# Attention and a routed expert layer in one program: the Router's chain in pieces between heads, halving on GpSimd, fewer row sends in the drain

## The reference, cut to what matters

```python
x = layernorm(x + attention(x))          # 16 heads, softmax(q k^T / sqrt(8)) v, then Wo, bo
# expert layer on N = 4096 tokens
shared = gelu(xf @ Wfc_s + bfc_s) @ Wproj_s + bproj_s
probs = softmax(xf @ Wr)                 # 8 experts
topk_p, topk_i = top_k(probs, 2); topk_p /= sum(topk_p)
routed = sum over the 2 chosen e: topk_p * (gelu(xf @ Wfc[e] + bfc[e]) @ Wproj[e] + bproj[e])
x = layernorm(x + shared + routed)
```

## Time and profile before

| | us |
|---|---|
| median of 3 runs | 584.2 |
| lowest and highest | 571.56, 597.54 |
| profiled execution, its own time | 578.29 |
| its span, first to last instruction | 576.5 |
| mean granted TensorE clock in it | 0.845 of full speed |

### The profile page before, as it was taken

How to read it: one execution, slowest core, us unless ns; L and a number is a source line. 1 busy time by engine, 2 the same in 40 slices (tenths; PEclk the granted TensorE clock), 3 DMA queues, 4 the chain that set the end, 5 groups by cost and what they waited for, 6 DMA issues and landing times. The chain is left out here.

```text
span 576.5 us, 14294 instructions
## 1 busy us (share of the span) xinstructions
PE 454.4 (79%) x5135; PEld 305.8 (53%) x5135; DVE 387.3 (67%) x873; ACT 306.9 (53%) x546; POOL 310.1 (54%) x417
## 2 busy tenths in 40 slices
PE   5998899989989887899992469991899999996000
PEld 2444454444545443344551358980699999995000
DVE  3658766696888787877721186550598999985095
ACT  1158755786888773545760366770444554452035
POOL 5322764466666631434678407881066666667185
PEclk9999956797999895656997589995899999999555
DMA  3234414453554431222121101114911111110263
GB/s 91 67 101 141 138 57 127 125 158 109 159 149 115 122 103 43 70 62 71 56 73 42 42 1 52 46 44 115 261 43 44 48 43 40 37 34 23 95 233 109
DMA packets 63127, 50.29 MB, mean 87 GB/s; under 512 B 7354, under 2 KB 54596, under 8 KB 63060
## 3 DMA queue, kind: packets, MB, share of 16 engines
q1 hardware_dynamic: 58516, 40.91, 25.4%
q0 software_dynamic: 4544, 8.47, 4.6%
HBM read 24.96 MB, written 22.95 MB: 83 GB/s over the span
## 5 line engine op out<-in xcount | busy, mean ns | idle before, releaser
L540 DVE TENSOR_REDUCE row_max<-s_ps 128x2 f32<-128x512 f32 x256 | 165.2, 684 | 57.4 <-PE s_ps L677 55.2
L400 ACT ACTIVATE probs<-ring_ps 128x1024 f32<-128x1024 f32 x128 | 130.9, 1023 | 76.5 <-PE ring_ps L695 76.2
L1573 POOL DMA_INDIRECT results<-gated,dest x78 | 78.8, 1010 | 63.3 <-DVE gated L1674 50.2
L677 PE MATMUL s_ps<-qk_stack 24*128 24x256 f16 x512 | 96.1, 302 | 18.7 <-DVE row_max L540 12.2
L1645 ACT ACTIVATE hid_r<-h_ps_r,bias 128x256 f32<-128x256 f32 x156 | 61.1, 474 | 74.5 <-PE h_ps_r L1309 74.5
L695 PE MATMUL ring_ps<-qk_stack 26*128 26x256 f16 x512 | 95.7, 303 | 0.0
L1276 POOL DMA_INDIRECT slots<-rows,slot_at x64 | 70.5, 1101 | 38.3 <-issue 17.5
L713 PE MATMUL av_ps<-probs,v_aug 128*32 128x256 f32 x1024 | 84.5, 457 | 0.0
L677 PEld LDWEIGHTS s_ps<-qk_stack 24*128 24x128 f16 x512 | 37.9, 99 | 79.0 <-issue 37.0
L310 POOL TENSOR_SCALAR max_scaled<-row_max 128x16 f32<-128x16 f32 x32 | 6.6, 205 | 104.2 <-DVE row_max L540 103.9
L1321 PE MATMUL y_ps_r<-w,hid_r 128*128 x312 | 58.1, 220 | 0.0
(11 more groups left out here) (208 smaller groups left out, 1060.3 us busy)
## 6 DMA issues: line engine op xcount, KB each, us to landing
qk_stack<-qk_rows SPq DMA_DIRECT2D x64, 96.0 KB
slots<-empty_row SPq DMA_DIRECT2D x13, 390.0 KB, 5.2
qk_rows<-qk_parts SPq DMA_DIRECT2D x16, 256.0 KB, 2.6
experts<-results SPq DMA_DIRECT2D x8, 512.0 KB, 6.9
rows_in<-slots SPq DMA_DIRECT2D x3, 1040.0 KB, 11.2
w_stage<-in_w_fc SPq DMA_DIRECT2D x9, 256.0 KB, 3.1
w_stage<-in_w_proj SPq DMA_DIRECT2D x9, 256.0 KB, 3.7
x_t<-in_x_t SPq DMA_DIRECT2D x16, 128.0 KB, 2.3
```

Source lines behind the costliest of these rows:

```text
L400: nc.scalar.activation(probs[:, n % PROBS], ring(key), ACT.Exp, scale=SCORE_SCALE).then_inc(ring_emptied, 1)
L540: nc.vector.tensor_reduce(row_max[:, h], s1_ps[:, h % 2], AX_X, ALU.max, negate=True).then_inc(max_done, 1)
L677: mm = nc.tensor.matmul(s1_ps[:, h % 2, t], band_of(q_stack, b, h, TERM_ROWS)[:, t * P:(t + 1) * P], band_of(k_stack, b, h, TERM_ROWS), st ...
L1573: nc.gpsimd.indirect_dma_start(out=a["results"][:, :], out_offset=bass.IndirectOffsetOnAxis(ap=dest[:, t.buf, half:half + 1], axis=0), in_ ...
```

## The change

1. The chain for share 0 is cut into pieces of one to four instructions and put between pairs of heads: `find`, `mark`, `settle` (together the old `pick`) for both choices in step 13; `tally`, `claim`, `offset` (the old `reserve`), `order`, `jump` (the old `rank`) and `gate` in step 14; `place(0, 0)`, `place(0, 1)`, `shift_on` and `end_on` (the old `move_on`) in step 15. `gap` is now made after `chosen`. PE's count moves from p = 6 of step 13 to p = 1 of step 14, ACT's `take_counts` and `share_gap` to step 14.
2. `make_x1` multiplies by 64: the variance with its eps is scaled by 1/4096 before the power of -1/2. So `x1_all` holds 64 x1. `cut_rows` needs no factor and moves to POOL, at the end of odd steps 5 to 19, all eight groups. The shared sum divides by `W_UNIT`, as do the gates, and the last layer norm's eps is multiplied by 4096.
3. Loads, casts and splits of the nine experts' weights are at listed steps, the shared expert's first: casts in 3, 4, 5, 7, 9, 11, 12, 13, 15, splits one later for each.
4. 17 instead of 30 sends stand in the attention block (3 in step 15, 5 in 16, 5 in 17, 4 in 18, none in 19), 47 instead of 34 in `share_and_place`.
5. In steps 13 to 16, PE runs `keep_clock(2)` after `project_v` (p = 2) and at p = 6.

```diff
-COUNT_STEPS = {13: 0}
+PICK_STEP, COUNT_STEP, PLACE_STEP = 13, 14, 15
-PLACED = {14: (0, 2), 15: (2, 2), 16: (2, 2), 17: (2, 4), 18: (4, 4), 19: (4, 2)}
+PLACED = {15: (0, 3), 16: (2, 3), 17: (2, 3), 18: (2, 2)}
+WEIGHT_ORDER = (8, 0, 1, 2, 3, 4, 5, 6, 7)
+CAST_AT = (3, 4, 5, 7, 9, 11, 12, 13, 15)
+SPLIT_AT = (4, 5, 6, 8, 10, 12, 13, 14, 16)
+LOAD_AT = (2, 3, 4, 6, 8, 10, 11, 12, 14)
+KEPT = range(13, 17)
...
 def halved_in(t):
-    return turned_in(t + 1)
+    g = (t - 5) // 2
+    return g if t % 2 == 1 and 0 <= g < GROUPS else None
...
             def make_x1(b):
-                nc.gpsimd.tensor_scalar(var_eps[:], mean_var[:, :, 1], EPS, None, ALU.add).then_inc(scale_done, 1)
+                nc.gpsimd.tensor_scalar(var_eps[:], mean_var[:, :, 1], EPS, X_UNIT ** -2, ALU.add, ALU.mult).then_inc(scale_done, 1)
...
             (POOL's step)
                 if last.exists():
                     add_bias(last)
+                if halved_in(t) is not None:
+                    halve(halved_in(t))
                 placer.send(PLACED.get(t, (0, 0))[1])
...
             (DVE's step, after heads 0 to 3 and take_mean)
-                if t in COUNT_STEPS:
-                    logits_taken(COUNT_STEPS[t])
-                    router.pick(COUNT_STEPS[t], 0)
-                if t == 14:
+                if now.exists():
+                    largest(now, 4)
+                    largest(now, 5)
+                if t == PICK_STEP:
+                    logits_taken(0)
+                    router.find(0, 0)
+                if t == COUNT_STEP:
                     counts_taken(0)
-                    router.reserve(0)
+                    router.tally(0)
+                if t == PLACE_STEP:
+                    router.place(0, 0)
                 if now.exists():
-                    for h in range(4, 8):
-                        largest(now, h)
...
+                    largest(now, 6)
+                    largest(now, 7)
+                if t == PICK_STEP:
+                    router.mark(0)
+                if t == COUNT_STEP:
+                    router.claim(0)
+                if t == PLACE_STEP:
+                    router.place(0, 1)
                 if last.exists():
                     invert_sums(last)
                     normalise(last)
...  (then, after heads 9, 11, 13 and 15:
      step 13: settle(0, 0); find(0, 1); mark(0); settle(0, 1)
      step 14: offset(0); order(0); jump(0); gate(0)
      step 15: shift_on(0); end_on(0))
...
             (PE's step)
+                    if p == COUNT_AT and t == COUNT_STEP:
+                        count(0)
...
                         project_v(now)
-                        if not last.exists():
+                        if not last.exists() or t in KEPT:
                             keep_clock(2)
...
                             turn_heads(last)
-                        elif now.exists():
+                        if now.exists() and (t in KEPT or not last.exists()):
                             keep_clock(2)
...
-def cut_rows(nc, dve, a, g):
+def cut_rows(nc, pool, a, g):
     tiles = slice(g * GROUP, (g + 1) * GROUP)
     parts = a["rows1"][:].bitcast(F16)
-    nc.vector.tensor_scalar(parts[:, tiles, 0:D], a["x1_all"][:, tiles], X_UNIT, 1.0, ALU.mult, ALU.mult)\
-      .then_inc(a["x_high"], 1)
-    dve.wait_ge(a["x_high"], g + 1)
-    nc.vector.scalar_tensor_tensor(out=parts[:, tiles, D:2 * D], in0=a["x1_all"][:, tiles], scalar=X_UNIT,
-                                   in1=parts[:, tiles, 0:D], op0=ALU.mult, op1=ALU.subtract).then_inc(a["x_low"], 1)
+    nc.gpsimd.tensor_scalar(parts[:, tiles, 0:D], a["x1_all"][:, tiles], 1.0, 1.0, ALU.mult, ALU.mult).then_inc(a["x_high"], 1)
+    pool.wait_ge(a["x_high"], g + 1)
+    nc.gpsimd.tensor_tensor(parts[:, tiles, D:2 * D], a["x1_all"][:, tiles], parts[:, tiles, 0:D], ALU.subtract)\
+      .then_inc(a["x_low"], 1)
...
             (share_and_place, DVE)
-            cut_rows(nc, dve, a, LAST_GROUP)
             low(0)
```

More of the change, by code:

```diff
@@ L365, in split_biases, with halve @@
                 pool.wait_ge(a["weights_low"], 2)
+            def halve(g):
+                pool.wait_ge(x1_made, 4 * g + 4)
+                cut_rows(nc, pool, a, g)
             placer = Placer(nc, pool, a)
@@ L473, in step @@
                     exp_pair(late, 1)
+                if t == COUNT_STEP:
+                    take_counts(0)
+                if late.exists():
                     evacuate_max(late, 1)
@@ L621, in step @@
                 if now.exists():
[L622 to L628, removed]
-                if halved_in(t) is not None:
-                    halve(halved_in(t))
-                if now.exists():
-                    for h in range(12, HEADS):
-                        largest(now, h)
+                    largest(now, 8)
+                    largest(now, 9)
+                if t == PICK_STEP:
+                    router.settle(0, 0)
+                if t == COUNT_STEP:
+                    router.offset(0)
+                if t == PLACE_STEP:
+                    router.shift_on(0)
+                if now.exists():
+                    largest(now, 10)
+                    largest(now, 11)
+                if t == PICK_STEP:
+                    router.find(0, 1)
+                if t == COUNT_STEP:
+                    router.order(0)
+                if t == PLACE_STEP:
+                    router.end_on(0)
+                if now.exists():
+                    largest(now, 12)
+                    largest(now, 13)
+                if t == PICK_STEP:
+                    router.mark(0)
+                if t == COUNT_STEP:
+                    router.jump(0)
+                if now.exists():
+                    largest(now, 14)
+                    largest(now, 15)
+                if t == PICK_STEP:
+                    router.settle(0, 1)
+                if t == COUNT_STEP:
+                    router.gate(0)
             run_steps(step)
@@ L1168, in pick, with mark, settle @@
         TE = [P, n, EXPERTS]
[L1169 removed]
+        best, score = a["best"][:, :, 0:n], a["score"][:, 0:n]
         of = a["logits"][:, tiles] if k == 0 else a["rest"][:, 0:n]
         if k == 1:
[L1172 removed]
+            then(nc.vector.scalar_tensor_tensor(out=of, in0=a["hot"][:, 0, tiles], scalar=FAR_BELOW, in1=a["logits"][:, tiles],
                                                 op0=ALU.mult, op1=ALU.add))
         then(nc.vector.tensor_reduce(best[:, k], of, AX_X, ALU.max))
[L1175 to L1176 removed]
         then(nc.vector.tensor_tensor(score, of, best[:, k].unsqueeze(2).to_broadcast(TE), ALU.is_equal))
[L1178 to L1180 removed]
+    def mark(self, c):
+        nc, a, then = self.nc, self.a, self.then
+        n = SHARES[c][1] - SHARES[c][0]
+        score, first = a["score"][:, 0:n], a["first"][:, 0:n]
+        then(nc.vector.tensor_tensor(score, score, a["from_end"][:].unsqueeze(1).to_broadcast([P, n, EXPERTS]), ALU.mult))
+        then(nc.vector.tensor_reduce(first, score, AX_X, ALU.max))
+    def settle(self, c, k):
+        nc, a, then = self.nc, self.a, self.then
+        tiles, n = slice(*SHARES[c]), SHARES[c][1] - SHARES[c][0]
+        hot, best, score, first = a["hot"], a["best"][:, :, 0:n], a["score"][:, 0:n], a["first"][:, 0:n]
+        then(nc.vector.tensor_tensor(hot[:, k, tiles], score, first.unsqueeze(2).to_broadcast([P, n, EXPERTS]), ALU.is_equal))
         if k == 1:
             then(nc.vector.tensor_tensor(a["chosen"][:, tiles], hot[:, 0, tiles], hot[:, 1, tiles], ALU.add), a["chosen_made"])
+            then(nc.vector.tensor_tensor(a["gap"][:, tiles], best[:, 1], best[:, 0], ALU.subtract), a["gap_made"])
+    def pick(self, c, k):
+        self.find(c, k)
+        self.mark(c)
+        self.settle(c, k)
     def gate(self, c):
@@ L1189, in gate @@
         dve.wait_ge(a["gap_exp"], c + 1)
-        then(nc.vector.tensor_scalar(gate1, exp_gap, UNIT, UNIT, ALU.mult, ALU.add))
+        then(nc.vector.tensor_scalar(gate1, exp_gap, W_UNIT, W_UNIT, ALU.mult, ALU.add))
         then(nc.vector.reciprocal(gate1, gate1))
@@ L1231, in rank @@
         then(nc.vector.tensor_tensor(rank, rank, over, ALU.add))
+    def rank(self, c):
+        self.order(c)
+        self.jump(c)
     def place(self, c, k):
@@ L1248, in move_on, with end_on @@
         then(nc.vector.tensor_tensor(a["shift"][:, c + 1], a["shift"][:, c], more[:], ALU.add))
+    def end_on(self, c):
+        nc, a, then = self.nc, self.a, self.then
+        some, more = a["some"], a["more"]
         then(nc.vector.scalar_tensor_tensor(out=more[:], in0=a["passing"][:, c], scalar=float(BLOCK), in1=some[:], op0=ALU.mult,
```

121 lines of the change are left out of this document (59 added, 62 removed).

## The result

| | us |
|---|---|
| median before, 4 runs | 581.03 (571.56 to 597.54) |
| median after, 4 runs | 547.31 (543.63 to 551.06) |
| ratio | 0.952, 95% interval 0.937 to 0.968 |
| profiled execution after, its span | 545.12, 543.4 |
| mean granted clock, after and before | 0.896, 0.845 |

The changed kernel is faster by 5%. The forecast, 565 us, had the direction and the two places; the measured median lies 18 us under it, 0.7 us under the low end of its range. The undisturbed medians are 574.7 us before and 547.3 after, 27.4 apart.

A forecast was written before the change was run, and what follows sets the result against it. TensorE at half clock was taken to bound the Router steps, POOL the drain and shared block. Terms -9.5 + 1.2 + 2.3 - 11 - 1.5 = -18.5 took the profiled 578.3 to 559.8 us; median forecast 565, range 548 to 581.

The forecast's parts named there:

- Part 1: Attention block's drain: sends in steps 17 to 19 fall from 20 to 9, halving added on POOL; -9.5 us, bounds -7 to -11.
- The layout: POOL's new drain queue laid out from 293.66 us, ending with halve(7) at 313.0 against 322.46.
- +1.2 for POOL's queue: Step 16's split_weights(8) and an extra send make POOL late for step 17's first splits: +1.2 us (0 to 3.2).
- Part 2: Shared expert's block: 15 sends of share 0 stand first instead of 2, mostly in an existing wait; +2.3 us (0 to 5.2).
- POOL bounds that block: Shared expert's block: POOL sends until 392.47, DVE's last add ends at 390.67; POOL bounds by some 2 us.
- Part 3: Steps 13 to 16, chain in pieces so the clock mostly holds: -11 us, from -15.1 (bounds -10.7 to -18.9).
- rival C: The port: each of 15 pieces meets a POOL instruction and waits 0.9 us more, 13.5 us; time 570 (576); chance 0.07.
- Part 4: The rest: halving leaves DVE in odd steps, weights' work spread; -1.5 us over four or five steps (0 to -4).
- Signs: What would show each part: POOL's drain end 9 us nearer, last send after 72 us, steps of 16 to 18 us.
- A: Rival: one long fall of the clock stays, half of part 3 is lost; 565.3 us (571 scaled to the median); chance 0.20.
- B: Rival: clock at half through steps 13 to 15, part 3 is 0, drain alone gives; 570.8 us (577); chance 0.15.
- D: Rival, slower: POOL late in steps 12 to 16, PE waits and its clock falls; about 580 or 589 (595); chance 0.10.

The follow-up runs named there:

- short_drain: The kernel before with only the drain's sends cut to 5 in step 17, 4 in 18, none in 19: 560.2 us, ratio 0.972.
- lumps: The changed kernel with each part of the chain in one lump between heads in the same steps 13 to 15: 561.8 us, undisturbed 556.6.
- balanced: The changed kernel without blank matmuls, the chain over four steps instead of three: 560.4 us, 9.1 less than before on this chip.
- pieces_only: The kernel before with only the chain in pieces and x1 times 64: 634.0 us on a slower chip, 4.9 less than before there.
- again: The changed kernel unedited, run once more on the first group's chip: 549.2 us, undisturbed 549.0.
- no_blanks: The changed kernel without the blank matmuls of steps 13 to 16: 543.5 us, undisturbed 543.4.

## Why the prediction was right, and where it was not

**Part 1, the drain.** Forecast -9.5; measured -10.6, and 24.7 us of short_drain against 36.8 shows it alone. The price of halving (1.9 for a pair with handshakes) and the send (1.26) held. The layout came out 1.1 us too long because of one of its terms: batch 15 was not bound to 308.4 us "in any case". In the trace of before DVE's last add_residual had waited 3.24 us for POOL's `add_bias`, which stood behind the same sends:

```profile
307.19 0.42 DVE L561 TENSOR_TENSOR z<-misc_ps,xb 128x256 f32<-128x256 f32 x1 [3.24 <-POOL xb L333]
```

With fewer sends its statistics ended 21.4 us after the first split of step 17, not 22.7, and POOL took them up 0.2 us later (283.49). In short_drain the same instruction waited for PE, no longer for POOL, and they ended after 21.9 us. The way into the next block, held constant, was 2.4 us instead of 3.5. Of the +1.2 for POOL's queue the cause is there, not the cost: in step 17 the first split starts at 261.96, 0.6 us after DVE's last maximum ended, just as worked out, but a longer step from it is not visible.

**Part 2, the shared block.** Forecast +2.3; from POOL's first send to the last, 290.50 to 358.35 against 325.97 to 392.47, +1.4. The wait for the slots went, as said. But "POOL bounds that block" may be half the truth: in after DVE's last add ends at 357.8, half a microsecond before POOL's last send. What bounds the block once the wait is gone, and whether still more sends there would cost in full, no run tested.

**Part 3, steps 13 to 16.** Forecast -11 + 1.2; measured 14.6 + 16.7 + 19.2 + 18.1 = 68.6 us from split to split for the four windows of the earlier trace rows that took 81.6, so -13.0, and the rest of the stretch to step 17, 5.3 us for 6.8, gives 1.5 more. The first two windows have the clock at 1.00, the last two 0.76 and 0.88, since one fall of 13.6 us stands across their seam:

```profile
228.00:229.00 1.00, 0.61 (x10) 0.22 (x8) 0.96 (x4) 0.23 (x1) 0.05 (x1) 1.00 0.58 176
229.00:242.60 13.60, 13.39 (x95) 6.07 (x99) 10.57 (x30) 7.34 (x11) 6.71 (x14) 0.51 0.21 58
```

lumps shows that the size of the pieces counts, 7.7 us undisturbed. That the clock then held through two and a half steps was in part luck: balanced and pieces_only have the same pieces in step 13 and fell there. The port, weighed as rival C with 13.5 us, cost 0.5 us twice (L1209, L1273) and 0.2 once (L1224) in steps 12 to 14. So the rule of the Trainium skill (SBUF — State Buffer, Who interferes with whom) agrees with the trace, and few pieces met a POOL instruction. The prediction took it to speak against this change; by the runs it speaks no less against the lumps, two of which lost 1.2 us each to POOL in lumps. (The bounds of this part add up to -10.6 and -19.3, not -10.7 and -18.9; nothing hangs on that.)

**Part 4, the term that was mis-sized.** Forecast -1.5, measured -9.2 (197.28 to 188.11). The term was priced by the quiet steps only, those at full clock, and there too it was small by more than half. Two quiet windows of after stand against the two of the earlier trace rows at clock 1.00:

```profile
146.20:159.83 13.63, 12.49 (x155) 6.75 (x156) 11.56 (x23) 11.75 (x18) 11.10 (x17) 1.00 0.45 117
159.83:174.07 14.24, 13.46 (x169) 7.38 (x169) 11.85 (x24) 11.17 (x19) 6.18 (x13) 1.00 0.57 153
```

That is 13.6 and 14.2 us where before took 14.15 and 14.70, 0.5 each, which over the eight windows from step 4 to 12 is 4. The two sources overlap: with halving back on DVE (halve_dve) the windows are 14.15 and 14.3, with the old weights (weights_old) 13.3 and 14.6. So over the eight windows halving gave 2.3 to 3.6 us and the spread of the weights 0.1 to 1.4, by the order in which they are undone.

The rest is the clock, 0.85 before and 0.93 after, for which the prediction had no term. The same instructions ran at 0.85 and 0.91 (before and short_drain), and kernels with x1 kept 64-fold at 0.90 to 0.99 in the eight profiles of the result and the first two groups; the one profile of before is the lowest of all, and from an execution with a low mean clock (0.845). Whether the change makes the falls in these steps rarer, or the profile of before was only an unlucky one, these runs do not settle. Against the undisturbed medians the gain is 27.4 us, against the profiles 33.1; the forecast was 18.5.

**Signs.** POOL's last instruction of the attention block came 9.2 us nearer to DVE's last statistics, as asked (9). The last send ended 70.2 us after the block before, where 72 was said and 70.0 was measured before. The steps took 14.6 to 19.2 us, not 16 to 18.

**Rivals.** A (one long fall stays, 571) did happen in its mechanism, 13.6 us at half speed, but not at its price. B (clock low through steps 13 to 15) did not; balanced, with two falls of 18 and 30 us, comes nearest to it. D (POOL late, slower) did not happen: the splits in steps 12 to 16 left the clock alone until 229 us, and weights_old, without them there, is 26.1 us under before, the change 19.8 (again) and 27.4.

**The range.** Its low end, 548, was built from part 3 at its best and the lower of the runs. It names nothing for steps 4 to 12, though the three runs of before, 26 us apart, had shown what the clock alone can do.

## What to carry to other kernels

Where two engines feed each other through two buffers, work that a third party needs goes between them in pieces no longer than the buffers cover; the lump can cost more than its length: in lumps TensorE stood for 3.4 and 2.8 us and came back at half speed. In a pipeline's drain, look for the engine that still works when the others have ended, and move what the next stage will wait for anyway into that wait. Before pricing an edit by one profile, ask how much of that profile is the clock: here one kernel's executions lie 26 us apart, more than most edits are worth. And before calling an engine's finish a floor, look whether its last instruction waited for the engine that you are about to relieve.

## What the runs showed of the hardware

The granted clock fell after far shorter stops of TensorE than I had expected: after 0.24 us busy in one microsecond (balanced, 206 us), and in after with 0.61 us busy in the microsecond before the fall at 229. But such a stop does not always bring it: no_blanks had the first of them as well, 1.15 us long, and kept its clock. Once down, it stayed down for 14, 18 and 30 us under nearly full load in the three places shown (in the second 17.43 of 18.00 us busy, at 0.53).

A send on POOL lasts 0.96 us alone and 1.31 when DVE's 128x512 subtraction of two SBUF tiles recurs beside it; then sends are 1.61 us apart from start to start, in step with the shared expert's tiles.
